# Inverting 16x16 diagonal blocks on POOL, reached by DMA, in a DeltaNet layer's kernel

## The chip, the cores and the metric

One core of a Trainium2 chip runs the whole layer. The metric is device time in microseconds of one execution; lower is better.

## The reference

The layer adds to its input an attention branch (a chunkwise delta rule, a multi-scale convolution and gates that mix them) and a feed-forward branch. Input and output are 2 x 4096 x 512, in float32; there are 4 heads of 128. The part that matters here is the delta rule: inside each chunk a unit lower triangular matrix is inverted by forward substitution.

```python
attn = -jnp.einsum('bhncd,bhned->bhnce', kbc, kc) * strict_lower
for i in range(1, chunk):
    upd = jnp.einsum('...j,...ji->...i', attn[..., i, :], attn[..., :, :i])
    attn = attn.at[..., i, :i].add(upd)
attn = attn + jnp.eye(chunk, dtype=q.dtype)
u = attn @ vc
w = attn @ kbc
```

The reference uses chunks of 32. The result does not depend on the size of the chunk but for rounding, and the kernel takes 128 tokens as a chunk.

## The kernel before, in words

The 4096 tokens of each of the 2 sequences (NB) are cut into NS = 32 steps of 128 tokens. The five engine programs, one function each (`sync_program`, `pool_program`, `tensor_program`, `scalar_program`, `vector_program`), are loops `for i in range(NS + 2)` in which step i is projected and transposed (f), step i - 1 is worked on in the middle (k) and step i - 2 is finished (c). Inside the loop every engine has its calls in an order that is written out by hand or by a planner, one call after another; for VectorE (DVE) this is down to single taps of the 31-tap convolution, `taps(s, h, lo, hi)`. Engines meet through semaphores alone. An engine never passes a call that waits.

A step has eight matrices (2 sequences x 4 heads) of 128x128. TensorE (PE) forms the Gram matrices K K^T in `gram` (L471), ScalarE (ACT) scales them into Bm in `scale_B` (L924), signal B_done. From Bm the inverse X of the unit triangular matrix is built in levels. Within 32x32 blocks there are five levels, block sizes 1 to 16. Level l is `inverse_W(s, l)` (L486): for eight matrices and four row groups a 32x32 by 32x16 product into the bank `inv`; on DVE `mask_W` (L1420) masks it into Wq; `inverse_Z(s, l)` (L509) multiplies by the transposed inverse so far, Xq; `step_Y` (L1428) subtracts the result from Yq, the inverse so far; and `turn_Y` (L1410) transposes Yq into Xq again. Level 0 needs no Z. Two more levels, from 32 to 64 (`inverse_W(s, 5)`, `copy_W`, `inverse_Z(s, 5)`, `spread_X`, `join_X`) and from 64 to 128 (`half_W`, `half_X`), complete X. X is used in `solve` (L557), which needs `subtract_state` and ends in u.

A float32 matmul of the program is two MATMUL records in the trace, so one W or Z pass of 32 matmuls is x64 there. PE does the level passes between other work: projections of the next step (`project`, L429), the transposes of x and of tokens (`turn_x`, `turn_tokens`), the last transposes of the output (`turn_o`) and its product (`attend`).

GpSimd (POOL) computes small powers: 1/sqrt for the layer norm (`deviation`), for q and k (`norms_q`, `norms_k`) and for the output norm (`invert_o`, L377). It also issues two sorts of accumulating DMA: `add_taps` (L385), which adds a product that ACT wrote into prod to my, and `add_out` (L390). SyncE (SP) issues loads: the weights, x of a step (`load_x`, L323), and a copy of x from DRAM to DRAM into the output (`copy_x`, L328), to which `add_out` adds.

Of the kernel before, what the change touches and what calls it, by code (L numbers as in the profile page):

```python
# [29 lines left out]
LEVELS = [1 << i for i in range(5)]  # L30
NL = len(LEVELS)
# [5 lines left out]
C_IDQ = C_LEV + NL * Q // 2  # L37
C_PART = C_IDQ + Q
# [35 lines left out]
def build(nc, x, out, w):  # L74
    NS = x.shape[1] // P
    with ExitStack() as ctx:
# [37 lines left out]
        def level_mask(l):  # L114
            k = LEVELS[l]
            m = cst[:, C_LEV + l * Q // 2:C_LEV + (l + 1) * Q // 2].rearrange("p (n k) -> p n k", k=k)
            return m[:, None, :, :].broadcast_to([P, NB * H, Q // 2 // k, k])

        def even(t, k):
            return t.rearrange("p (n k) -> p n k", k=2 * k)[:, :, 0:k]  # L120

        def evens(t, k):
            return t.rearrange("p b h (n k) -> p (b h) n k", k=2 * k)[:, :, :, 0:k]

        def ones_of(i):
            one = cst[:, C_IDQ:C_IDQ + Q].rearrange("p (n k) -> p n k", k=2)[:, :, i]
            return one[:, None, :].broadcast_to([P, NB * H, Q // 2])
# [17 lines left out]
        YW = sb("YW", P, NB, H, HP)  # L145
        S = sb("S", P, NB, D)
# [65 lines left out]
        def each_head(t):  # L212
# [27 lines left out]
        ones_in = signal("ones_in")  # L240
        W_mm, W_done, Wo_done = signal("W_mm", NL + 1), signal("W_done", NL), signal("Wo_done")
        Y_turned, X_spread, Z_mm, Y_done = (
            signal("Y_turned", NL), signal("X_spread"), signal("Z_mm", NL), signal("Y_done", NL))
# [40 lines left out]
        def sync_program(e):  # L284
# [48 lines left out]

            load(cst_in, cst[:, :], w["cst"])
# [4 lines left out]
            load_rest()  # L339
            for i in range(NS + 2):  # L340
                if 2 <= i < NS:
                    load_x(i)
                if 1 <= i <= NS:
                    copy_x(i - 1)
            for i in range(2):
                e.wait_ge(stored[i], NS // 2 * 16)

        def pool_program(e):
# [27 lines left out]

            def invert_o(s, b):  # L377
# [18 lines left out]
            for i in range(NS + 2):  # L396
# [10 lines left out]
                if k:  # L407
                    add_taps(i - 1, 3, 2)
                    add_taps(i - 1, 3, 3)
                    norms_q(i - 1)  # L410
                    norms_k(i - 1)
                if c:
                    add_out(i - 2)

        def tensor_program(e):
# [70 lines left out]
            def inverse_W(s, l):  # L486


                if l == 0:
                    e.wait_ge(*B_done.upto(s))  # L490
                    e.wait_ge(*aT_done.upto(s, 0))
                else:
                    e.wait_ge(*Y_done.upto(s, l - 1))
                for j in range(NB * H):
                    b, h = divmod(j, H)
                    if l < NL:
                        k, n = LEVELS[l], Q // 2
                        for r in range(4):
                            yv = Yq[rows(r), b, h, :] if l else cst[rows(r), C_IDQ:C_IDQ + Q]
                            i = e.matmul(inv[rows(r), j * n:(j + 1) * n].rearrange("p (n k) -> p n k", k=k),  # L500
                                         Bm[rows(r), b, h * P + r * Q:h * P + (r + 1) * Q], even(yv, k), start=True, stop=True)
                    else:
                        for r in (0, 2):
                            i = e.matmul(inv[rows(r + 1), j * Q:(j + 1) * Q],
                                         Bm[rows(r), b, h * P + (r + 1) * Q:h * P + (r + 2) * Q], Yq[rows(r), b, h, :],
# [270 lines left out]
        def scalar_program(e):  # L776
# [393 lines left out]
            for i in range(NS + 2):  # L1170
# [9 lines left out]
                if f:  # L1180
                    sum_x(i)
# [662 lines left out]
```

## Time and profile before

| what | us |
|---|---|
| median of the runs | 3586.57 |
| lowest and highest of 3 runs | 3575.02, 3588.57 |
| span of the profiled execution, first to last instruction | 3583.2 |
| PE busy | 3454.6 |
| DVE busy | 3199.5 |
| ACT busy | 2765.0 |
| POOL busy | 423.0 |

The time of the profiled execution itself is not given apart from its span; the median of the runs stands 3.4 us above the span. A row of the page's groups gives line, engine, operation, what is written and read, the count, then busy time in us and the mean of one in ns, and behind the last bar the idle time before them with what ended it. Line numbers are those of the kernel before.

### The profile page before, as it was taken

What the parts mean: (1) busy time and instruction counts of PE and PEld (TensorE: products, weight loads), DVE (VectorE), ACT (ScalarE), POOL (GpSimd) and SP (SyncE); (2) the same over time, 40 slices, a digit from 0 to 9 for tenths busy, and PEclk for the clock granted to TensorE, in tenths of its full rate; (3) what the DMA queues carried; (4) which work ended last, traced back from release to release, by engine and by line L of the source; (5) the groups of instructions that cost most, each with busy time, mean ns of one, the idle gap of its engine ahead of it and who ended that gap; (6) DMA issues with size and microseconds to landing.
All of it is one profiled execution on the core that took longest, in us unless ns stands there. A gap on an engine that the chain in (4) does not pass through costs nothing. (4 is left out here: it accounts for less than half of the span.)

```text
span 3583.2 us, 97697 instructions
## 1 busy us (share of the span) xinstructions
PE 3454.6 (96%) x37184; PEld 2572.7 (72%) x37184; DVE 3199.5 (89%) x8208; ACT 2765.0 (77%) x9176; POOL 423.0 (12%) x497
## 2 busy tenths in 40 slices
PE   6999999999999999999999999999999999999986
PEld 5677777777777777777777777777777777777764
DVE  6998898998989999989999989989999998899983
ACT  5677887778887778887788877788877788777774
POOL 1011100111100111101111001111001110011110
PEclk9999999999999999999999999999999999999988
DMA  5022111122111122111221111221112221112110
GB/s 177 5 41 42 35 31 28 31 41 42 30 32 25 38 42 40 31 28 26 41 42 37 30 28 31 41 41 30 32 22 41 42 38 29 31 27 41 36 26 10
DMA packets 52204, 131.04 MB, mean 37 GB/s; under 512 B 9389, under 2 KB 9901, under 8 KB 51481
## 3 DMA queue, kind: packets, MB, share of 16 engines
q0 software_dynamic: 31744, 79.70, 12.9%
q1 hardware_dynamic: 19992, 45.10, 3.7%
q8 instruction: 294, 4.82, 0.6%
q14 instruction: 174, 1.42, 0.1%
HBM read 45.09 MB, written 33.55 MB: 22 GB/s over the span
## 5 line engine op out<-in xcount | busy, mean ns | idle before, releaser
L1488 DVE SCALAR_TENSOR_TENSOR my<-vT,mw,my 128x256 f32<-128x256 f32 x5408 | 2230.9, 480 | 105.6 <-ACT my L1054 69.9
L645 PE MATMUL dense<-xsh,w 128*128 128x256 f32 x2048 | 481.9, 381 | 1.3
L645 PEld LDWEIGHTS dense<-xsh,w 128*128 128x128 f32 x2048 | 368.3, 190 | 68.9 <-ACT xr L1116 8.3
L388 POOL DMA_DIRECT2D my<-prod x160 | 141.8, 886 | 964.6 <-ACT my L1054 498.4
L439 PE MATMUL front<-xsh,wk 128*128 128x256 f32 x1024 | 239.9, 387 | 3.4 <-ACT raw L835 3.4
L439 PE MATMUL front<-xsh,wv 128*128 128x256 f32 x1024 | 240.9, 388 | 0.8 <-ACT xsh L812 0.8
L586 PE MATMUL dense<-xk,wfk 128*128 128x256 f32 x1024 | 239.5, 387 | 0.0
L357 POOL TENSOR_SCALAR vare<-xsq 128x2 f32<-128x2 f32 x32 | 6.1, 192 | 1951.3 <-ACT xsh L797 1951.3
L678 PE MATMUL dense<-wo,ms 128*128 128x512 f32 x512 | 235.7, 604 | 0.0
L598 PE MATMUL dense<-wr,xr 128*128 128x512 f32 x512 | 233.7, 599 | 1.2 <-DVE xb L1471 1.2
L1065 ACT ACTIVATE prod<-vT,mw 128x256 f32<-128x256 f32 x480 | 210.3, 511 | 28.2 <-DMA my<-prod 27.9
L439 PE MATMUL front<-xsh,wq 128*128 128x256 f32 x1024 | 231.9, 379 | 0.0
L602 PE MATMUL dense<-wfv,ka 128*128 128x512 f32 x512 | 230.2, 592 | 0.0
L623 PE MATMUL dense<-cm,ym 128*128 128x512 f32 x512 | 225.0, 592 | 0.0
L439 PEld LDWEIGHTS front<-xsh,wq 128*128 128x128 f32 x1024 | 191.9, 190 | 38.8 <-issue 14.8
L990 ACT ACTIVATE Bm<-cell,g 128x128 f32<-128x128 f32 x256 | 73.0, 368 | 184.7 <-PE cell L561 184.7
L439 PEld LDWEIGHTS front<-xsh,wk 128*128 128x128 f32 x1024 | 190.1, 190 | 29.9 <-ACT raw L835 3.5
L439 PEld LDWEIGHTS front<-xsh,wv 128*128 128x128 f32 x1024 | 190.7, 191 | 27.9 <-issue 1.4
L586 PEld LDWEIGHTS dense<-xk,wfk 128*128 128x128 f32 x1024 | 190.3, 191 | 27.0
L614 PE MATMUL small<-my,km 128*128 128x256 f32 x768 | 201.8, 400 | 2.2 <-issue 2.2
L1054 ACT ACTIVATE my<-vT,mw 128x256 f32<-128x256 f32 x384 | 167.4, 507 | 36.2 <-PE small L614 35.9
L602 PEld LDWEIGHTS dense<-wfv,ka 128*128 128x128 f32 x512 | 97.2, 190 | 122.5 <-issue 108.6
(181 smaller groups left out, 6897.8 us busy)
## 6 DMA issues: line engine op xcount, KB each, us to landing
my<-prod POOLq DMA_DIRECT2D x160, 384.0 KB, 4.1
xa<-in_x SPq DMA_DIRECT2D x32, 512.0 KB, 4.2
out<-xb POOLq DMA_DIRECT2D x32, 512.0 KB, 5.9
w<-in_w SPq DMA_DIRECT2D x1, 2048.0 KB, 17.1
wv<-in_wv SPq DMA_DIRECT2D x1, 1024.0 KB, 6.6
wk<-in_wk SPq DMA_DIRECT2D x1, 1024.0 KB, 8.9
wq<-in_wq SPq DMA_DIRECT2D x1, 1024.0 KB, 8.4
wfk<-in_wfkT SPq DMA_DIRECT2D x1, 1024.0 KB, 7.1
```

Of the source, the lines that this page charges most:

```text
L388: e.dma_start(my[h % 2][:, :, :], prod[:, :, :], accum_op=ALU.add).then_inc(taps_added, 16)
L439: i = e.matmul(by_batch(front[pair % 2][:, c * W:(c + 1) * W]), wt[:, k, hs(c0 + c)], xsh[s % 2][:, k, :, 1:1 + P], start=(k == 0), stop=( ...
L586: i = e.matmul(dense[pair][:, c * W:(c + 1) * W], wfk[:, k, hs(2 * pair + c)], xk[:, k, :], start=(k == 0), stop=(k == CB - 1))
L598: i = e.matmul(dense[0][:, :], xr[:, k, hs(b)], wr[:, k, :], start=(k == 0), stop=(k == CB - 1))
L602: i = e.matmul(dense[1][:, :], ka[:, k, hs(b)], wfv[:, k, :], start=(k == 0), stop=(k == CB - 1))
L614: i = e.matmul(s_mix, km[:, p, :], my[h % 2][:, p, :], start=(p == 0), stop=(p == 2))
L623: i = e.matmul(dense[b][:, :], ym[:, k, hs(b)], cm[:, k, :], start=(k == 0), stop=(k == CB - 1))
L645: e.matmul(by_batch(o), w1[:, k, hs(2 * pair + c)], xsh[s % 2][:, k, :, 1:1 + P], start=(k == 0), stop=False)
L678: i = e.matmul(dense[b][:, :], ms[:, b, hs(h)], wo[:, h, :], start=(h == 0), stop=(h == H - 1))
L1054: i = e.activation(by_batch(my[h % 2][:, p, :]), vT[s % 2][:, c, :, VH - TAPS[j] + 1:VH - TAPS[j] + 1 + P], ACT.Copy, scale=mw[:, WOFF[j] ...
L1065: i = e.activation(by_batch(prod[:, p, :]), vT[s % 2][:, c, :, off:off + P], ACT.Copy, scale=mw[:, col:col + 1])
L1488: i = e.scalar_tensor_tensor(o, vT[s % 2][:, c, :, off:off + P], mw[:, col:col + 1], o, ALU.mult, ALU.add)
```

## The change

The levels 1, 2, 4 and 8 of the inversion leave TensorE. Each 16x16 diagonal block (8 in each of 8 matrices, so 64, named UNITS) goes to one partition of its own and is inverted there on POOL by substitution. The way is through two new DRAM tensors whose matrices lie 129 rows apart, so that the diagonal blocks are evenly spaced:

```diff
+            def units(t):
+                each = t.rearrange("j p c -> (j p c)").rearrange("(m x) -> m x", x=UPITCH)
+                return each[:, 0:HQ * P].rearrange("m (r c) -> m r c", c=P)[:, :, 0:HQ]
...
+            def write_rows(s, b):
+                e.wait_ge(*B_done.upto(s, b))
...
+                e.dma_start(rows_out[b * H:(b + 1) * H, 0:P, :].rearrange("j p c -> p j c"), heads(Bm, b)).then_inc(rows_written, 16)
+            def read_rows(s):
+                e.wait_ge(rows_written, 16 * NB * (s + 1))
...
+                e.dma_start(Bu[:, :, :], units(rows_out)).then_inc(rows_read, 16)
+            def write_units(s):
+                e.wait_ge(*units_done.upto(s))
...
+                e.dma_start(units(units_out), Xu[:, :, :]).then_inc(units_written, 16)
+            def read_units(s):
+                e.wait_ge(units_written, 16 * (s + 1))
...
+                for r in range(4):
+                    e.dma_start(each_head(Yq)[rows(r), :, :],
+                                units_out[:, r * Q:(r + 1) * Q, r * Q:(r + 1) * Q].rearrange("j p c -> p j c")).then_inc(units_read, 16)
```

All of these are issued from SP. Its order in a pass of the loop is now:

```diff
+            zero_units()
             for i in range(NS + 2):
-                if 2 <= i < NS:
-                    load_x(i)
+                if 1 <= i <= NS:
+                    write_rows(i - 1, 0)
+                    write_rows(i - 1, 1)
+                    read_rows(i - 1)
+                if 1 <= i < NS - 1:
+                    load_x(i + 1)
                 if 1 <= i <= NS:
                     copy_x(i - 1)
+                    write_units(i - 1)
+                    read_units(i - 1)
```

POOL's part has 14 pairs of a product and a subtraction, of up to 56 elements in each of 64 partitions, and waits for each of its own results. It stands behind the DMA add of (3, 0) and ahead of that of (3, 1):

```diff
+            def invert_units(s):
+                def then(ins):
+                    e.wait_ge(*unit_step.link(ins))
+                e.wait_ge(rows_read, 16 * (s + 1))
...
+                then(e.tensor_tensor(Xu[:, :, :], Bu[:, :, :].rearrange("m j i -> m i j"), minus_lower, ALU.mult))
+                then(e.memset(Xu[:, :, :].rearrange("m i c -> m (i c)")[:, 0:HQ * HQ:HQ + 1], 1.0))
+                for j in range(1, HQ - 1):
+                    n = HQ - 1 - j
+                    then(e.tensor_tensor(Tu[:, 0:n, 0:j], Bu[:, j, j + 1:HQ][:, :, None].broadcast_to([UNITS, n, j]),
+                                         Xu[:, j, 0:j][:, None, :].broadcast_to([UNITS, n, j]), ALU.mult))
+                    left = e.tensor_tensor(Xu[:, j + 1:HQ, 0:j], Xu[:, j + 1:HQ, 0:j], Tu[:, 0:n, 0:j], ALU.subtract)
+                    if j < HQ - 2:
+                        then(left)
+                left.then_inc(units_done.sem, 1)
...
                     add_taps(i - 1, 3, 0)
+                    invert_units(i - 1)
                     add_taps(i - 1, 3, 1)
```

On PE one W and one Z pass are left (`inverse_W(s)`, waiting for units_read, and `inverse_Z(s)`), followed by `join_W` and `join_Z`, which were level 5. On DVE `turn_Y` runs twice, `mask_W` and `step_Y` once; ACT no longer writes ones into Yq:

```diff
-            def turn_Y(s, l):
+            def turn_Y(s, n):
+                if n:
+                    e.wait_ge(*Y_done.upto(s))
+                else:
+                    e.wait_ge(units_read, 64 * (s + 1))
...
-                e.transpose(flat(Xq), flat(Yq)).then_inc(Y_turned.sem, 1)
+                e.transpose(flat(Xq), flat(Yq)).then_inc(Y_turned.sem, 1)
```

The scratch of the software DMA queues is set to 8192 bytes. The orders of PE, ACT and DVE are all written anew. On PE, the calls from ffn_key(0) to solve(0) that opened a pass of the loop now close the one before, with key_state(0) ahead of solve(1). Of the order tables one line shows the kind:

```diff
-                    mask_W(i - 1, 3)
+                    taps(i - 1, 2, 39, 40)
```

PE from the second transpose of x to the third Z pass, in a pass of the loop before. cell<-qT,kT is query_key, front<-cst,xa turn_x, cell<-Yq,Bm a W pass, cell<-Wq,Xq a Z pass, cell<-S,kT key_state, small<-my,km kernel_mix, front<-xsh a projection:

```order
L426 MATMUL front<-cst,xa 128x128 x4
L500 MATMUL cell<-Yq,Bm 32x16 x32
L554 MATMUL cell<-S,kT 128x128 x4
L521 MATMUL cell<-Wq,Xq 32x16 x32
L614 MATMUL small<-my,km 128x256 x3
L500 MATMUL cell<-Yq,Bm 32x16 x32
L439 MATMUL front<-xsh,wv 128x256 x8
L521 MATMUL cell<-Wq,Xq 32x16 x32
L439 MATMUL front<-xsh,wv 128x256 x8
L500 MATMUL cell<-Yq,Bm 32x16 x32
L439 MATMUL front<-xsh,wk 128x256 x8
L521 MATMUL cell<-Wq,Xq 32x16 x32
```

The same place in the changed kernel, from the two query_key products to the one Z pass (turn<-cst,vT is turn_tokens, dense<-cst,dl turn_o):

```order
L545 MATMUL cell<-qT,kT 128x128 x8
L675 MATMUL small<-my,km 128x256 x3
L488 MATMUL front<-cst,xa 128x128 x4
L530 MATMUL turn<-cst,vT 128x128 x4
L615 MATMUL cell<-S,kT 128x128 x4
L501 MATMUL front<-xsh,wv 128x256 x16
L501 MATMUL front<-xsh,wk 128x256 x16
L530 MATMUL turn<-cst,vT 128x128 x4
L731 MATMUL dense<-cst,dl 128x128 x4
L555 MATMUL cell<-Yq,Bm 32x16 x32
L731 MATMUL dense<-cst,dl 128x128 x4
L566 MATMUL cell<-Wq,Xq 32x16 x32
```

The passes between the projections are gone, and the one W pass stands behind all four projections and the first turn_o.

DVE in the changed kernel, from the two masked attention matrices aT (`make_aT`) to the transpose that waits for units_read, the mask and the first subtraction; dl<-dl are the additions of the output's parts (`add_two`, `add_three`), my<-vT,mw,my are taps:

```order
L1440 TENSOR_TENSOR aT<-cell,cst 128x512 x2
L1515 SCALAR_TENSOR_TENSOR my<-vT,mw,my 128x256 x13
L1565 TENSOR_TENSOR dl<-dl,ms 128x512
L1515 SCALAR_TENSOR_TENSOR my<-vT,mw,my 128x256 x7
L1570 TENSOR_TENSOR dl<-dl,y 128x512
L1515 SCALAR_TENSOR_TENSOR my<-vT,mw,my 128x256 x2
L1565 TENSOR_TENSOR dl<-dl,ms 128x512
L1515 SCALAR_TENSOR_TENSOR my<-vT,mw,my 128x256
L1570 TENSOR_TENSOR dl<-dl,y 128x512
L1515 SCALAR_TENSOR_TENSOR my<-vT,mw,my 128x256 x17
L1453 STREAM_TRANSPOSE Xq<-Yq 128x256
L1460 TENSOR_TENSOR Wq<-cell,cst 128x128
```

Before, the first of five transposes stood directly behind the second aT.

SP in the changed kernel, the DMAs of one pass of the loop, with the semaphores that each waits for:

```order
L343 DMA rows_out<-Bm 128x4x128 [waits rows_read,B_done] x2
L349 DMA Bu<-rows_out 64x16x16 [waits units_done,rows_written]
L321 DMA xa<-in_x 128x2x512 [waits x_turned]
L327 DMA out<-in_x 2x4x16384
L357 DMA units_out<-Xu 64x16x16 [waits units_read,units_done]
L366 DMA Yq<-units_out 32x8x32 [waits Y_turned,X_spread,W_mm,units_written]
L366 DMA Yq<-units_out 32x8x32 x3
```

Before, only the load of x and the copy of x stood there.

## Rows read from the trace of the kernel before

**Rows 1.** The page's head and part 1, busy us (share of the span) and instructions.

```profile
span 3583.2 us, 97697 instructions
PE 3454.6 (96%) x37184; PEld 2572.7 (72%) x37184; DVE 3199.5 (89%) x8208; ACT 2765.0 (77%) x9176; POOL 423.0 (12%) x497
```

**Rows 2.** Timeline of PE (start us, us, ...), features' first transpose, steps 1 and 31.

```profile
154.58 0.22 PE L631 MATMUL small<-ident,fparts 128*108 128x128 bf16 x1
...
3425.14 0.27 PE L631 MATMUL small<-ident,fparts 128*108 128x128 bf16 x2
```

**Rows 3.** Groups by line, PE, Z and W passes of the levels.

```profile
L521 PE MATMUL cell<-Wq,Xq 32*32 32x16 f32 x8192 | 98.1, 182 | 24.1 <-issue 15.6 <-DVE Wq L1426 8.2
L500 PE MATMUL cell<-Yq,Bm 32*32 32x16 f32 x8192 | 97.3, 181 | 15.3 <-issue 12.1 <-DVE Yq L1438 2.8 <-DVE Yq L1434 0.3
```

**Rows 4.** Timeline of PE, a W pass between projections, and an attend.

```profile
1721.53 0.72 PE L500 MATMUL cell<-Yq,Bm 32*32 32x16 f32 x64
1722.19 3.73 PE L439 MATMUL front<-xsh,wk 128*128 128x256 f32 x16
...
1731.74 3.60 PE L678 MATMUL dense<-wo,ms 128*128 128x512 f32 x8
```

**Rows 5.** Timelines of ACT and PE, the second scaled Gram matrix and small groups.

```profile
1704.20 1.14 ACT L931 ACTIVATE Bm<-cell,g 128x128 f32<-128x128 f32 x4
...
1700.38 1.53 PE L614 MATMUL small<-my,km 128*128 128x256 f32 x6
...
1758.77 1.06 PE L554 MATMUL cell<-S,kT 128*128 128x128 f32 x8
```

**Rows 6.** Groups by line, DVE, transposes, masks and subtractions of the levels.

```profile
L1415 DVE STREAM_TRANSPOSE Xq<-Yq 128x256 f32<-128x256 f32 x160 | 70.2, 439 | 0.0
L1426 DVE TENSOR_TENSOR Wq<-cell,cst 128x128 f32<-128x128 f32 x160 | 44.8, 280 | 5.0 <-PE cell L500 4.9
L1438 DVE TENSOR_TENSOR Yq<-Yq,cell 128x128 f32<-128x128 f32 x128 | 36.2, 283 | 20.9 <-PE cell L521 20.9
```

**Rows 7.** DMA issues (KB each, us to landing), and SP's timeline of one.

```profile
km<-in_km SPq DMA_DIRECT2D x1, 192.0 KB, 2.5
mw<-in_m SPq DMA_DIRECT2D x1, 62.0 KB, 4.0
mu<-in_mu_k SPq DMA_DIRECT2D x1, 2.0 KB, 1.8
...
15.84 0.43 SPq L286 DMA_DIRECT2D mu<-in_mu_k  x1
```

**Rows 8.** Timelines of POOL and DVE, POOL beside taps and beside a resting DVE.

```profile
1723.25 0.48 DVE L1488 SCALAR_TENSOR_TENSOR my<-vT,mw,my 128x256 f32<-128x256 f32 x1
1723.38 0.40 POOL L379 TENSOR_SCALAR oe<-so 128x4 f32<-128x4 f32 x1
...
3561.47 0.18 POOL L379 TENSOR_SCALAR oe<-so 128x4 f32<-128x4 f32 x1 [70.23 <-ACT y L1156]
3561.73 1.03 POOL L383 TENSOR_TENSOR rro<-oe,cst 128x4 f32<-128x4 f32 x1
...
1745.19 9.19 DVE L1488 SCALAR_TENSOR_TENSOR my<-vT,mw,my 128x256 f32<-128x256 f32 x23
```

**Rows 9.** PE's timeline in the last step; busy time by stretch (us, then PE, PEld, DVE, ACT, POOL busy, PEclk, DMA share, GB/s).

```profile
3460.86 1.05 PE L521 MATMUL cell<-Wq,Xq 32*32 32x16 f32 x64 [1.92 <-DVE Wq L1426]
3464.75 1.05 PE L500 MATMUL cell<-Yq,Bm 32*32 32x16 f32 x64 [2.83 <-DVE Yq L1438]
3469.85 1.05 PE L521 MATMUL cell<-Wq,Xq 32*32 32x16 f32 x64 [4.05 <-DVE Wq L1426]
...
3476.20 4.28 PE L678 MATMUL dense<-wo,ms 128*128 128x512 f32 x8
...
1700.00:1810.00 110.00, 107.69 (x1168) 80.21 (x1168) 99.90 (x259) 86.88 (x288) 13.44 (x16) 1.00 0.17 34
3460.00:3470.00 10.00, 2.26 (x141) 2.10 (x145) 9.96 (x26) 9.86 (x38) 4.46 (x6) 0.53 0.45 81
```

More of the change, by code:

```diff
@@ L29 @@
 Q = 32
-LEVELS = [1 << i for i in range(5)]
-NL = len(LEVELS)
+HQ = Q // 2
+NU = P // HQ
+UNITS = NU * NB * H
+PITCH = (P + 1) * P
+UPITCH = HQ * (P + 1)
 WOFF = [0, TAPS[0] * CB, (TAPS[0] + TAPS[1]) * CB]
@@ L682, in tensor_program @@
                 f, k, c = i < NS, 1 <= i <= NS, i >= 2
-                if c:
-                    turn_tokens(i - 2, 3)
-                    inverse_Z(i - 2, 5)
-                    ffn_key(i - 2, 0)
-                    half_W(i - 2)
-                    ffn_key(i - 2, 1)
-                    half_X(i - 2)
-                    ffn_out(i - 2, 0)
-                    solve(i - 2, 1)
-                    key_state(i - 2, 0)
-                    kernel_mix(i - 2, 2)
-                    solve(i - 2, 0)
                 if k:
@@ L731, in tensor_program @@
                     kernel_mix(i - 1, 0)
+                    gram(i - 1, 0)
                     gram(i - 1, 1)
-                    query_key(i - 1, 0)
                 if f:
@@ L736, in tensor_program @@
                 if k:
-                    turn_tokens(i - 1, 2)
-                    inverse_W(i - 1, 0)
+                    query_key(i - 1, 0)
                     query_key(i - 1, 1)
+                    kernel_mix(i - 1, 1)
                 if f:
@@ L773, in tensor_program @@
                 if k:
-                    inverse_W(i - 1, 5)
+                    join_Z(i - 1)
+                    ffn_key(i - 1, 0)
+                    half_W(i - 1)
+                    ffn_key(i - 1, 1)
+                    half_X(i - 1)
+                    ffn_out(i - 1, 0)
+                    key_state(i - 1, 0)
+                    solve(i - 1, 1)
+                    kernel_mix(i - 1, 2)
+                    solve(i - 1, 0)
         def scalar_program(e):
@@ L1556, in vector_program @@
                 if c:
+                    taps(i - 2, 3, 4, 5)
+                    taps(i - 2, 3, 2, 4)
+                    taps(i - 2, 3, 7, 8)
+                    taps(i - 2, 3, 5, 6)
+                    taps(i - 2, 3, 10, 11)
+                    taps(i - 2, 3, 6, 7)
+                    taps(i - 2, 3, 13, 14)
+                    taps(i - 2, 3, 9, 10)
+                    taps(i - 2, 3, 8, 9)
+                    taps(i - 2, 3, 16, 17)
                     taps(i - 2, 3, 12, 13)
-                    taps(i - 2, 3, 10, 11)
+                    taps(i - 2, 3, 19, 20)
@@ L1702, in vector_program @@
                 if k:
-                    taps(i - 1, 2, 16, 17)
+                    taps(i - 1, 2, 29, 30)
+                    taps(i - 1, 2, 18, 19)
                 if c:
@@ L1706, in vector_program @@
                 if k:
-                    taps(i - 1, 2, 19, 20)
+                    taps(i - 1, 2, 16, 17)
                 if c:
@@ new lines, in vector_program @@
+                    taps(i - 1, 2, 45, 46)
+                    turn_Y(i - 1, 0)
+                    mask_W(i - 1)
+                    taps(i - 1, 2, 46, 47)
+                    taps(i - 1, 2, 33, 34)
+                    taps(i - 1, 2, 47, 48)
+                    taps(i - 1, 2, 28, 29)
+                    taps(i - 1, 2, 48, 49)
+                    taps(i - 1, 2, 36, 37)
+                    step_Y(i - 1)
+                    taps(i - 1, 2, 49, 50)
+                    turn_Y(i - 1, 1)
+                    taps(i - 1, 2, 50, 51)
```

565 lines of the change are left out of this document (263 added, 302 removed).

## The prediction

> **What bounds the kernel now.** I read the page's totals first [rows 1]: PE is busy 3454.6 of 3583.2 us (96%), DVE 3199.5 (89%), and the others less. PE is nearly full and in its own order, so a step of the pipeline costs what PE issues in it plus what PE waits for. The timeline of PE gives the step [rows 2]: the first transpose of features (L631) starts at 154.58 and, 30 steps later, at 3425.14, so a step is 3270.56 / 30 = 109.0 us. Then I read PE's groups by line [rows 3] for what the inversion costs there, PE's timeline at the passes [rows 4], and the timelines of ACT, DVE and POOL for what the new way would cost [rows 5 to 8]. A difference under 0.5% (18 us) is about what a measurement of this kernel can't tell from none.
>
> **What goes from PE.** Five passes W of 64 instructions and four passes Z stand in each step; one of each stays. A pass holds PE from one start to the next: 1721.53 to 1722.19, that is 0.66 us [rows 4]. Seven passes are 7 x 0.66 = 4.6 us. PE also idles before these passes: 24.1 + 15.3 = 39.4 us in 32 steps [rows 3], 1.2 us a step, and a little before the first W; I take 1.1 us of it. The step would be 109.0 - 4.6 - 1.1 = 103.3 us if nothing took their place.
>
> **What goes from DVE and ACT.** Three of five transposes, four of five masks and all but one subtraction. By their groups [rows 6]: 3/5 of 70.2, 4/5 of 44.8 and 3/4 of 36.2 are 105.1 us, and the first subtraction of each step, another 32 of the last kind, makes it 114 us or 3.6 us a step. ACT loses the ones that it wrote into Yq, under half a microsecond. Neither engine is the bound, so this buys room alone. The larger order tables redistribute taps and other work; I cost the move of the first ten PE calls from the head of one pass of the loop to the end of the one before at nothing, since the same instructions stand in the same sequence (only key_state(0) and solve(1) change places). The added buffers' zeroing is one DMA in the first 45 us of loads, where PE waits anyway.
>
> **What comes: one long chain.** From the second scaled gram (B_done) to the first pass W everything is now serial: Bm to DRAM, the blocks to 64 partitions, POOL, the inverses to DRAM, and four DMAs to Yq. Its price, link by link:
> - *Bm out*, 256 KB. No row shows a plain store from SBUF. The nearest load is 192 KB in 2.5 us; below stands 1.8 for 2 KB, above 4.0 [rows 7]. I take 2.6.
> - *Blocks in*, 64 KB in 1024 runs of 64 bytes. The floor is 1.8 us, a 2 KB load; above is 4.0, a 62 KB load of 512 short runs that stood behind others [rows 7]. I take 3.0.
> - *Inverses out*, the same runs: 3.0, same bounds.
> - *Inverses in*, four DMAs, issued one by one. An issue takes 0.43 us (mu_k's on SP [rows 7]), so the last starts after 1.3 and lands 2.1 later: 3.4. Bounds: 1.3 + 1.8 and 1.3 + 4.0.
> - *Between them*, four semaphores at about 0.1 each: 0.4.
> - *POOL*: a product over 256 elements, a memset, then 28 operations in pairs, each waiting for the one before. The nearest small POOL operation is TENSOR_SCALAR: 0.18 us while DVE rests, but 0.40 while DVE runs taps, and it ends 0.05 us after the tap that was running (tap 1723.25 to 1723.73, POOL done 1723.78) [rows 8]. The next dependent one starts 0.08 later (3561.65 to 3561.73). So a dependent POOL operation gets one opening per tap, and taps follow each other every (9.19 - 0.48) / 22 = 0.396 us [rows 8]. 28 x 0.40 = 11.2, plus 1.1 for the first two: 12.3. Bounds: undisturbed, 28 x (0.18 + 0.08) + 0.6 = 7.9; two taps for each, 28 x 0.79 + 1.5 = 23.6. I take the middle value because rows 8 show exactly this waiting, on operations as short.
>
> Sum 2.6 + 3.0 + 12.3 + 3.0 + 3.4 + 0.4 = **24.7 us**, between 15 and 40 at the ends.
>
> The Trainium skill, "DMA: Bandwidth & Descriptors", section "Anatomy of one DMA", puts about 2.0 us of fixed cost on a DMA and little on 64 KB, but its "Specifications" add read-modify-write under 512 bytes. By the fixed cost alone the estimate of the four links is 2.6 + 2.2 + 2.2 + 3.5 = 10.5 us, 1.5 less than mine, and the total some 45 us lower; the second rule speaks against this change, and no row here shows a short store.
>
> **What covers it.** ACT ends the second scaled gram at 1704.20 + 1.14 = 1705.34 [rows 5]. By the new order PE then has up to the first pass W: kernel_mix 1.53; half of query_key, turn_x, turn_tokens, key_state, turn_tokens and turn_o, six small groups of 128x128 matmuls of which the fullest takes 1.06 and the halves about 0.5, 3.6 in all; and four projections at 3.73, which overlap their neighbours by some 0.08, 14.6 [rows 4, 5]. That is 19.7 us. So PE waits 24.7 - 19.7 = **5.0 us** in each step. DVE's order agrees: 40 taps and four additions stand between the last aT and the transpose that waits for the same DMAs, 40 x 0.396 + 4 x 0.6 = 18.2 us; behind that transpose DVE's taps wait too, in the room that [rows 6] give and DVE's idle 384 us. Part of the 5 us comes already at turn_o: POOL's third product add, both inverse roots of o and so ACT's normalize_o are queued behind the 30 POOL instructions. SP's load and copy of x stand between blocks in and inverses out, but they issue while POOL computes.
>
> **What the wait costs beside itself.** In the last step, where PE idles 2 to 4 us before passes [rows 9], the granted clock was 0.53 between 3460 and 3470, nearly all of it at 1.2 GHz in place of 2.4, and the attend group that follows takes 4.28 us, against 3.60 in a full step [rows 4, 9]. In a full step it is 1.00 [rows 9]. I add 1.5 us a step for matmuls behind the wait at the lower level; bounds 0 and 3.6.
>
> **Sum.** 103.3 + 5.0 + 1.5 = 109.8, or +0.8 us a step over 31 steps with cover: +25. In the last step no projections cover the chain: PE waits 14.6 more, while before it already waited for level passes, 1.92 to 4.05 before each of three, about 9 [rows 9], and later for the tap DMAs; I add 20 for it with the later tap adds. 3583 + 45 = 3628 us; the runs' median stands 3.4 above this span, and the profiled execution's own time isn't told apart, so I name **3630**, 1.2% above the median of 3586.57.
>
> **The rivals.**
> 1. *The chain fits, or nearly.* If POOL runs as while DVE rests (7.9) and the DMAs take 2 us each, the chain is under 20 and PE stays at 103.3: 3583 - 31 x 5.7 + 5 = 3411; with a wait of 3 us about 3505. For it: the removed 4.6 us are certain, and a wait under some 4 us leaves a gain. Against it: rows 8, DVE is never at rest there. Chance 0.33, all of it faster.
> 2. *The wait eats just the gain.* Wait and clock together between 4.6 and 5.7 us, which with the last step's 20 us is within 18 us of before. Chance 0.12.
> 3. *My forecast*, a net loss of 0.1 to 4.4 us a step, with the last step's 20 us 3605 to 3740: chance 0.38.
> 4. *DVE becomes the bound.* In a full step it is busy 99.90 of 110 us [rows 9], so 99.0 of 109.0, with 10 idle; without 3.6 busy and 0.8 of waits for passes it is 104.6. If each of 28 POOL operations held DVE off for its 0.18 and DVE waited 5.0 at the transpose, the step is 104.6 + 5.0 + 5.0 = 114.6, total 3583 + 31 x 5.6 + 20 = 3777. Against it: taps beside POOL's roots keep 0.48 [rows 8]. For it: these read far fewer elements than 40 on average. It decides from 0.18 us per operation. Chance 0.09. The Trainium skill, "SBUF — State Buffer", section "Who interferes with whom", says that a DVE instruction with two SBUF inputs and a GpSimd one that reads SBUF exclude each other for the whole instruction, whoever starts first. The trace agrees in one direction, POOL waiting for the tap (0.40 against 0.18); by that rule taps wait too, and it is this rival.
> 5. *POOL falls behind by a tap each time*: 23.6 in place of 12.3, wait 16.3, 3583 + 31 x 12.1 + 40 = 3998. Chance 0.08.
>
> So faster 0.33, same 0.12, slower 0.55. The range reaches from the chain that fits, 3410, to the edge of the DVE case, 3770; below and above lie rival 5 and the ends of the others.
>
> **What would show it.** Right: PE idle before the first pass W (and before turn_o), released by a DMA into Yq or by DVE's transpose, 3 to 8 us a step; POOL's 28 operations 0.32 to 0.42 us each; the two short-run DMAs landing in 2.5 to 3.5 us; taps still 0.48; granted clock under 1.00 in full steps. Wrong: steps of 103 to 105 us with no wait at W (rival 1); taps over 0.5 us and DVE busy over 3150 (rival 4); POOL operations at 0.8 (rival 5). Seven fewer passes and PE busy down by about 150 us should show in any case.

## The result, and the profile after

The changed kernel takes 3790.15 us (median of 4 runs, 3788.75 to 3791.78), beside 3587.51 us for the kernel before (4 runs): ratio 1.0575, 95% interval 1.0558 to 1.0591. It is slower, as forecast, by 203 us in place of 43, and 20 us above the upper end of the range. Of all executions in what follows, one of ten of the version with the roots of o earlier took 7909.89 us; why is not known, and the ratios leave it out.

The page's head and part 1 of the changed kernel:

```profile
span 3787.5 us, 69932 instructions
PE 3383.6 (89%) x22848; PEld 2490.8 (66%) x22848; DVE 3165.3 (84%) x7856; ACT 2761.4 (73%) x9144; POOL 813.6 (21%) x1457
```

Against [rows 1] PE issues 14336 matmuls fewer, yet its busy time falls by 71 us alone, and the span grows by 204.3. Measured from one first transpose of features to the next over 30 steps, as in [rows 2], a step is 115.4 us in place of 109.0. Summed over PE's timeline in those 30 steps, the idle time per step is 10.1 us, before 1.7; all figures "a step" below are taken this way. The waits view, PE and ACT (engine, line waited for: us in total, times, longest us):

```profile
PE dense L731 <- ACT dl L1203: 117.6, 24, 12.6
PE turn L530 <- ACT turn L945: 101.8, 23, 21.0
PE cell L555 <- DMA Yq<-units_out: 66.1, 27, 12.1
...
ACT dl L1203 <- POOL rro L443: 97.1, 24, 7.8
```

L731 is turn_o, L530 turn_tokens, L555 the first pass W. The three stand one behind another in PE's order, and a step has its wait at one or another of them. Two steps in PE's timeline:

```profile
1705.59 0.60 PE L530 MATMUL turn<-cst,vT 128*128 128x128 f32 x4
1714.01 1.12 PE L731 MATMUL dense<-cst,dl 128*128 128x128 f32 x4 [7.82 <-ACT dl L1203]
1716.72 1.05 PE L555 MATMUL cell<-Yq,Bm 32*32 32x16 f32 x64 [1.59 <-DMA Yq<-units_out]
...
1720.80 5.98 PE L739 MATMUL dense<-wo,ms 128*128 128x512 f32 x8
...
1727.33 3.70 PE L739 MATMUL dense<-wo,ms 128*128 128x512 f32 x8
...
1831.10 1.08 PE L530 MATMUL turn<-cst,vT 128*128 128x128 f32 x4 [7.31 <-ACT turn L945]
...
1833.22 1.05 PE L555 MATMUL cell<-Yq,Bm 32*32 32x16 f32 x64
```

In the first step PE waits 7.82 us at turn_o and 1.59 at W; in the second 7.31 us at turn_tokens, and then nothing. Together the three make 7.9 us a step. The first attend behind a wait takes 5.98 us, the second 3.70. The stretches of the second step (PE, PEld, DVE, ACT, POOL busy, PEclk, DMA share, GB/s) show the granted clock at 0.60 right behind the wait, most of it at 1.2 GHz:

```profile
1820.00:1830.00 10.00, 3.79 (x18) 2.98 (x16) 6.65 (x16) 4.36 (x22) 7.53 (x20) 0.89 0.24 48
1830.00:1840.00 10.00, 8.90 (x147) 5.82 (x148) 6.11 (x17) 8.86 (x29) 1.91 (x2) 0.60 0.41 71
```

POOL's timeline of that step: the second product add, the product with the mask, the memset, the first and the last of 28 operations, then the two kinds of work that queued behind them.

```profile
1809.99 0.86 POOL L448 DMA_DIRECT2D my<-prod  x1 [6.56 <-ACT my L1095]
1811.53 1.93 POOL L426 TENSOR_TENSOR Xu<-Bu,cst 64x256 f32<-64x256 f32 x1 [0.68 <-DMA Bu<-rows_out]
1813.52 0.12 POOL L427 MEMSET Xu<- 64x16 f32 x1
1813.72 0.50 POOL L430 TENSOR_TENSOR Tu<-Bu,Xu 64x14 f32<-64x14 f32 x1
1814.29 0.34 POOL L432 TENSOR_TENSOR Xu<-Xu,Tu 64x14 f32<-64x14 f32 x1
...
1826.08 0.32 POOL L432 TENSOR_TENSOR Xu<-Xu,Tu 64x14 f32<-64x14 f32 x1
1827.45 0.87 POOL L448 DMA_DIRECT2D my<-prod  x1 [1.05 <-ACT prod L1106]
1828.40 0.19 POOL L439 TENSOR_SCALAR oe<-so 128x4 f32<-128x4 f32 x1
```

From 1811.53 to 1826.40 the inversion takes 14.9 us. The DMA issues (KB each, median us to landing), and two of DVE's groups:

```profile
my<-prod POOLq DMA_DIRECT2D x160, 384.0 KB, 4.4
...
rows_out<-Bm SPq DMA_DIRECT2D x64, 256.0 KB, 3.5
...
Yq<-units_out SPq DMA_DIRECT2D x128, 32.0 KB, 2.0
...
Bu<-rows_out SPq DMA_DIRECT2D x32, 64.0 KB, 3.0
units_out<-Xu SPq DMA_DIRECT2D x32, 64.0 KB, 3.4
```

```profile
L1515 DVE SCALAR_TENSOR_TENSOR my<-vT,mw,my 128x256 f32<-128x256 f32 x5408 | 2233.8, 483 | 52.4 <-DMA my<-prod 40.9
...
L1453 DVE STREAM_TRANSPOSE Xq<-Yq 128x256 f32<-128x256 f32 x64 | 28.3, 442 | 218.7 <-DMA Yq<-units_out 218.7
```

Taps take 483 ns, as in the kernel before (0.48 in [rows 8]), so DVE isn't held off for whole operations. It waits 218.7 us at the transpose for the inverses, more than PE does at W.

Medians over 27 full steps, from the issue and landing times in the trace, give the chain from B_done: 0.4 to the second write's issue, 3.6 until it has landed, 3.0 blocks in, 14.8 POOL, 3.4 inverses out, 3.6 inverses in: 28.8 us. The first pass W starts 0.1 later, in all 29.0 us after B_done.

### The profile page after: what moved, and what is told of

The parts are those of the page before. It is cut to its first block, busy times and chain, and to the rows that moved or that the text cites. A ratio compares the mean times of both kernels' runs of the same rounds, so it can differ in the third digit from the quotient of the medians.

```text
span 3787.5 us, 69932 instructions
## 1 busy us (share of the span) xinstructions
PE 3383.6 (89%) x22848; PEld 2490.8 (66%) x22848; DVE 3165.3 (84%) x7856; ACT 2761.4 (73%) x9144; POOL 813.6 (21%) x1457
## 3 DMA queue, kind: packets, MB, share of 16 engines
q0 software_dynamic: 31744, 79.70, 12.3%
## 4 chain that ended last, share of the span: by engine, by line
PE 48%; ACT 20%; DMA 12%; POOL 9%; issue 8%; DVE 2%; SPq 1%; ACTq 0%; POOLq 0%; DVEq 0%
PE dense L739 8%; PE dense L706 6%; PE dense L647 6%; PE dense L659 6%; PE dense L663 6%; POOL Xu L432 4%; POOL Tu L430 4%; PE front L501 3%; DMA my<-prod 3%; DMA rows_out<-Bm 3%; DMA units_out<-Xu 2%; DMA Bu<-rows_out 2%; PE small L675 2%; ACT my L1095 2%; ACT dense L1125 2%
## 5 line engine op out<-in xcount | busy, mean ns | idle before, releaser
L739 PE MATMUL dense<-wo,ms 128*128 128x512 f32 x512 | 288.9, 716 | 0.0
L501 PE MATMUL front<-xsh,wv 128*128 128x256 f32 x1024 | 231.9, 384 | 15.1 <-ACT xsh L860 15.1
L501 PE MATMUL front<-xsh,wk 128*128 128x256 f32 x1024 | 226.7, 379 | 0.0
L501 PEld LDWEIGHTS front<-xsh,wq 128*128 128x128 f32 x1024 | 192.0, 190 | 38.8 <-issue 14.8
L1453 DVE STREAM_TRANSPOSE Xq<-Yq 128x256 f32<-128x256 f32 x64 | 28.3, 442 | 218.7 <-DMA Yq<-units_out 218.7
L739 PEld LDWEIGHTS dense<-wo,ms 128*128 128x128 f32 x512 | 113.0, 233 | 126.4 <-issue 123.9
L675 PE MATMUL small<-my,km 128*128 128x256 f32 x768 | 194.0, 389 | 1.5 <-DVE my L1515 1.5
```

Source lines behind the costliest of these rows:

```text
L501: i = e.matmul(by_batch(front[pair % 2][:, c * W:(c + 1) * W]), wt[:, k, hs(c0 + c)], xsh[s % 2][:, k, :, 1:1 + P], start=(k == 0), stop=( ...
L675: i = e.matmul(s_mix, km[:, p, :], my[h % 2][:, p, :], start=(p == 0), stop=(p == 2))
L739: i = e.matmul(dense[b][:, :], ms[:, b, hs(h)], wo[:, h, :], start=(h == 0), stop=(h == H - 1))
```

## The experiments

I began with two suspects. One is the chain. The other is SP's copy of x into the output: 512 KB in 8 packets of 64 KB, 2.4 us each and two at a time, about 10 us in all. Before the change they run 46 to 57 us after the step's first product add, clear of all five adds; now, placed behind the read of the blocks, they run at 12 to 22 us, beside the second add. That add then lands after 10 to 16 us in two thirds of the steps instead of 4, and ACT's next product waits for it, ahead of copy_tokens and so of turn_tokens. ACT's timeline in the second step above:

```profile
1825.60 1.31 ACT L1106 ACTIVATE prod<-vT,mw 128x256 f32<-128x256 f32 x3 [7.90 <-DMA my<-prod]
```

**The copy behind the chain.** The copy goes behind the reads of the inverses in SP's order.

```diff
-                    copy_x(i - 1)
                     write_units(i - 1)
                     read_units(i - 1)
+                    copy_x(i - 1)
```

> The changed kernel with SP's copy of x (DRAM to DRAM) issued after the four DMAs into Yq instead of before the inverses go out. Theory 1, the serial chain from the scaled gram to Yq (28 us against some 20 of cover) makes the wait: the waits of PE before turn_tokens, turn_o and W, 7.9 us a step together, fall by at most 2, the step stays 113 to 115.5 us, ratio to before 1.035 to 1.06. Theory 2, the copy's 64 KB packets hold DMA engines, the tap add (3, 0) lands after 10 to 16 us instead of 4 and ACT and PE wait for that: adds land in 4 to 6 us again and most of the 7.9 us goes, step 106 to 109, ratio 0.97 to 1.00. Both agree that the wait at turn_tokens (2.7 us a step on average) goes.

3923.42 us, ratio 1.0963 [1.0944, 1.0982], slower still. The copy's packets now run at 30 to 42 us, beside the fourth add, which lands after 12 to 13 us: some 110 of its 128 packets start in its first 4 us, the last ones only when the copy's last packet is through. Rows of PE's timeline:

```profile
1772.56 1.12 PE L731 MATMUL dense<-cst,dl 128*128 128x128 f32 x4 [6.00 <-ACT dl L1203]
1775.68 1.05 PE L555 MATMUL cell<-Yq,Bm 32*32 32x16 f32 x64 [2.01 <-DMA Yq<-units_out]
...
1794.89 1.14 PE L598 MATMUL cell<-YW,Bm 64*64 64x64 f32 x16 [1.41 <-ACT YW L1010]
```

The wait at turn_tokens is gone, as both theories had it, but 6.0 and 1.9 us a step stand at turn_o and W, the same sum. The collision moved to another place, where it costs a new wait, 2.2 us a step at L598 (join_W's product). Neither theory's time held.

**POOL's 28 operations left out.** In invert_units only the product and the memset remain, so the inverse is incomplete and only the time counts.

```diff
-                for j in range(1, HQ - 1):
...
-                left.then_inc(units_done.sem, 1)
```

> The changed kernel without POOL's 28 products and subtractions (the masked product and the memset stay), so the inverse is left incomplete. Theory 1: the chain is 13 us shorter, 15 to 16 us, and covered: no wait at turn_o or W, clock 1.00 in full steps, step 103 to 105.5, ratio 0.95 to 0.97. Theory 2: the tap add (3, 0) still lands after 10 to 16 us in two thirds of the steps and PE still waits about 7 us before turn_tokens in some of them, step 106 to 108, ratio 0.975 to 0.99.

3709.83 us, ratio 1.0346 [1.0314, 1.0379], step 113.2, above both expectations. Only 2 us a step are won by taking 13 us out of POOL's part of the chain. PE still waits 3.1 us a step at turn_tokens and 3.0 at W. The DMA issues say why:

```profile
units_out<-Xu SPq DMA_DIRECT2D x32, 64.0 KB, 12.6
```

The inverses are now written while the copy's packets still run on the same queue, and land after 12.6 us in place of 3.4. The inverses reach Yq only 3 us earlier.

**The copy moved in the kernel before.** There the copy alone is put where the change puts it.

```diff
-                if 2 <= i < NS:
-                    load_x(i)
+                if 1 <= i < NS - 1:
+                    load_x(i + 1)
                 if 1 <= i <= NS:
                     copy_x(i - 1)
```

> The kernel before with SP's copy of x issued right behind the next load of x, where the changed kernel has it, and nothing else. Theory 2: the tap add that runs beside it lands after 10 to 16 us, ACT waits for it, 0.5 to 4 us a step, ratio 1.005 to 1.04. Rival, POOL's new operations delay its own DMA's descriptors: adds land in 4 to 6 us here, ratio 0.995 to 1.005.

3712.42 us, ratio 1.0365 [1.0347, 1.0382]: the copy's place is able to cost 130 us in a kernel without any chain. The second add lands after 6 to 10 us there. ACT's timeline shows a product held 4.49 us by an add, and PE waits for ACT at the third projection:

```profile
1781.61 1.31 ACT L1065 ACTIVATE prod<-vT,mw 128x256 f32<-128x256 f32 x3 [4.49 <-DMA my<-prod]
```

```profile
PE front L439 <- ACT raw L835: 82.5, 30, 4.5
```

**POOL alone.** The same 30 operations once more at the program's start, on a zeroed Bu, while DVE rests.

```diff
+            probe()
             for i in range(NS + 2):
```

> The changed kernel with POOL's 30 operations run once more at its start, on zeros, while DVE rests. If taps of DVE stretch POOL's operations, as forecast from rows 8: here the product over 256 elements takes 0.6 to 0.9 us instead of 1.89, the 28 others 0.20 to 0.30 each, 28 with gaps 8 to 9.5 us instead of 13. If POOL's own pace sets them: the same as in the loop, 1.9 and 0.2 to 0.36, 12 to 13 us. The time itself changes by under 15 us either way.

3791.98 us in its one run. POOL's timeline:

```profile
4.38 0.84 POOL L463 TENSOR_TENSOR Xu<-Bu,cst 64x256 f32<-64x256 f32 x1
...
5.48 0.21 POOL L467 TENSOR_TENSOR Tu<-Bu,Xu 64x14 f32<-64x14 f32 x1
5.76 0.23 POOL L469 TENSOR_TENSOR Xu<-Xu,Tu 64x14 f32<-64x14 f32 x1
...
14.60 0.21 POOL L469 TENSOR_TENSOR Xu<-Xu,Tu 64x14 f32<-64x14 f32 x1
```

Alone the whole takes 14.81 - 4.38 = 10.4 us, in the loop 14.8. At the start the other engines rest too, so this run by itself does not name DVE; the loop does. Of the 896 operations of the 28 in the changed kernel's trace, 20 have no DVE instruction beside them and take 0.25 us on average, the others 0.38. So working beside DVE costs POOL 4.4 us a step. Undisturbed, POOL still needs 0.33 us per operation, start to start.

**The copy first.** The copy stands ahead of the first write of rows, so it goes once an older output is stored, as before the change.

```diff
                 if 1 <= i <= NS:
+                    copy_x(i - 1)
                     write_rows(i - 1, 0)
...
-                    copy_x(i - 1)
```

> The changed kernel with SP's copy of x put ahead of the first write of B's rows, so that it goes once the output two steps before is stored, clear of the five adds of the taps' products, as it did in the kernel before. POOL's inversion and all five transfers of the chain stay. Theory (two causes: the copy's place costs some 4 us a step, the chain the rest): the add (3,0) lands in 4 to 5 us again, PE's wait ahead of turn_tokens(3) falls under 1 us a step, the step is 111 to 113 us and the time 3640 to 3710, ratio to the kernel before 1.015 to 1.035. Rival (the chain of the inverses is all, the copy only took the blame): the wait stands ahead of W, Z or turn_o instead, 3760 to 3800, ratio 1.05 to 1.06. Rival (the prediction was right but for the copy): 3610 to 3650, ratio 1.01 to 1.02.

3788.74 us, ratio 1.0574 [1.0554, 1.0594]. The packets run at 52 to 63 us, the second add lands in 5 to 8 us, and nothing is won: the theory of two separate costs fell. PE's waits:

```profile
PE dense L731 <- ACT dl L1203: 200.9, 32, 12.6
PE cell L555 <- DMA Yq<-units_out: 68.5, 32, 11.5
```

The 7.9 us are all there, now in every step as 6.0 at turn_o and 1.9 at W.

**The copy in rows.** It stays in the change's place, but goes as 2 KB rows.

```diff
-                e.dma_start(out[:, s * P:(s + 1) * P, :], x[:, s * P:(s + 1) * P, :])
+                e.dma_start(out[:, s * P:(s + 1) * P, :].rearrange("b p d -> p b d"),
+                            x[:, s * P:(s + 1) * P, :].rearrange("b p d -> p b d"))
```

> The changed kernel with the copy of x at the same place, but cut into rows of 2 KB (128 tokens by 2 batches), where the changed kernel's copy moves 8 packets of 64 KB of some 2.4 us each. Theory (it is the few large packets, one behind another on few DMA engines, that hold back the packets of the add beside them): spread over 16 engines the copy takes 3 to 5 us, the add (3,0) lands in 4 to 8 us, ratio to the kernel before 1.02 to 1.04. Rival (bytes count, not packets: the memory or the engines are full for as long whatever the packets): the copy takes as long, the add lands after 10 to 16 us still, ratio 1.05 to 1.06. Rival (many small packets fill the queue ahead of the inverses' transfer): inverses out lands after 6 us or more, ratio over 1.06.

3782.41 us, ratio 1.0554 [1.0535, 1.0573]. The copy lands after 7.3 us, no add takes more than 8.3, the inverses out 3.4: the large packets do hold the others back, as the theory said, but its 1.02 to 1.04 missed, for their removal again changes only where PE waits. Two different cures of the copy leave the time as it was, within 8 us.

**Both taken away.** The copy first, and POOL's 28 operations left out, so the inverse is incomplete here too.

> The copy put first as in the run above, and POOL's 28 subtractions and products of the inversion left out (the blocks then hold the unit matrix minus B, not the inverse). Theory (copy's place and chain are the whole loss): both gone, the step is 103 to 105 us, the time 3410 to 3480, ratio to the kernel before 0.95 to 0.97. Rival (a third cost remains, such as the transfers of 64-byte runs beside the adds, or the order of the engines): a step over 107 us, ratio 0.98 or more.

3460.45 us, ratio 0.9656 [0.9640, 0.9672]. PE's timeline, where turn_o and W stood:

```profile
1669.40 0.66 PE L723 MATMUL dense<-cst,dl 128*128 128x128 f32 x4
1669.99 0.73 PE L547 MATMUL cell<-Yq,Bm 32*32 32x16 f32 x64
...
1672.03 0.71 PE L558 MATMUL cell<-Wq,Xq 32*32 32x16 f32 x64 [0.73 <-DVE Wq L1452]
```

No wait is left there but 0.73 us at Z for DVE's mask. The four kernels make a square (us a step):

| | copy in the change's place | copy first |
|---|---|---|
| all 28 operations | 115.4 | 114.9 |
| none | 113.2 | 104.8 |

Taking away one gives 0.4 or 2.1 us, both 10.6. Copy and chain are two ways to the same instructions of PE, about equally late, and the later one counts. They are not fully apart: without the operations, the copy in the change's place also holds up the chain itself, at the inverses out (12.6 us above). With the copy out of the way this run also measures the cover: its inverses land 15.2 us after the second write's issue, but W starts at 19.8, so PE has 19.8 + 0.4 = 20.2 us of work between B_done and W.

**Half of the operations.** The copy first, and only the last 7 pairs; the blocks are not fully inverted.

```diff
-                for j in range(1, HQ - 1):
+                for j in range(HQ // 2, HQ - 1):
```

> The copy of x first, and of POOL's 14 pairs only the last 7 (j from 8 to 14), so that the blocks aren't fully inverted. Theory (the wait is the chain minus a cover of 20.2 us from the second scaled gram to the first pass): 14 operations fewer at 0.46 us shorten the chain from 28.7 to 22.2 us, PE's waits at turn_o and W fall from 7.9 to some 2 us, the step is 106.5 to 108.5 us (114.9 with all pairs, 104.8 with none) and the ratio to the kernel before 0.98 to 1.00. Rival (the wait at turn_o is not the chain, but POOL's later work, the clock is most of the rest): step 104.8 to 106, ratio 0.965 to 0.975. Rival (something else holds the end): step 110 us or more.

3600.51 us, ratio 1.0049 [1.0033, 1.0064], step 109.3, above the 108.5 of the theory. The chain was nearly as computed (the inverses land 22.3 us after the second write's issue, 22.7 after B_done), and so were the waits:

```profile
PE cell L555 <- DMA Yq<-units_out: 74.3, 32, 6.5
PE dense L731 <- ACT dl L1203: 28.3, 13, 12.6
```

That is 2.7 us in a step of the loop. The rest goes with the clock. PE's step without its idle time, and the time at 1.2 GHz in the step, are 102.0 and 0.2 us without the wait, 104.5 and 6.4 here, 105.0 and 12.1 with all operations, the copy first in all three. Beside a wait of 2.7 us PE's own work takes 2.5 us longer, beside one of 7.9 us 3.0.

**POOL's other work put into the inversion.** The add (3,1) goes after 8 pairs, the roots of o, merged into one, after 10; PE, ACT and DVE keep their orders.

> The copy of x first, the whole inversion, and POOL's other work put into its middle: the add (3,1) after 8 of 14 pairs, both roots of o as one pair of operations after 10. PE, ACT and DVE keep their orders. Theory (the chain alone sets how long PE is late, the work queued behind it only says at which instruction): the wait at turn_o goes to under 1 us, that at W grows to 9 to 11 us since the chain is 2.9 us longer, the step is 116 to 118 us, ratio 1.065 to 1.085. Rival (the wait at turn_o is a cost of its own): step 109 to 111, ratio 1.0 to 1.02.

3885.78 us, ratio 1.0841 [1.0823, 1.0859], step 118.3.

```profile
PE cell L562 <- DMA Yq<-units_out: 244.1, 32, 12.7
PE dense L738 <- ACT dl L1210: 135.3, 32, 14.5
```

The chain grew by 3.2 us, the two waits by 3.4, the step by 3.4: what stands at turn_o is paid back at W. The theory had the time right and the places not: the wait at turn_o only fell to 3.9 us, not under 1, and that at W is 7.5, not 9 to 11.

**The passes later on PE.** Both turn_o, both attend and half of ffn_key go ahead of W; ACT's and DVE's orders follow.

```diff
+                    ffn_key(i - 1, 0, (0,))
                     inverse_W(i - 1)
+                    ffn_key(i - 1, 0, (1,))
                     inverse_Z(i - 1)
+                    ffn_key(i - 1, 1, (0,))
                     join_W(i - 1)
+                    ffn_key(i - 1, 1, (1,))
                     join_Z(i - 1)
...
                     half_W(i - 1)
...
                     half_X(i - 1)
+                    project(i, 4)
```

> The same POOL order, and the passes behind the chain put later on PE: both turn_o, both attend and half of ffn_key stand ahead of W, halves of ffn_key between the passes, the parts of ffn_out between the half passes, the fifth projection of the next step ahead of key_state, the second gate matmul ahead of outputs; ACT's and DVE's orders follow. Theory (the chain of 31.6 us then has a cover of 20.2 + 9.3 + 1.9 = 31.4 us): PE idles 2 to 4 us a step, the clock stays at the full one, the step is 104 to 107 us and the time 3430 to 3530, ratio 0.955 to 0.985, faster than both kernels. Rival (all later work of the step moves with the chain, since ACT and DVE are near full too): new waits of PE at key_state, solve or outputs, the step 109 us or more, ratio over 1.0.

3743.80 us, ratio 1.0446 [1.0431, 1.0462], step 113.6: 46 us better than the change, far off the 3430 to 3530 expected. No wait is left at the passes, since W starts 4 us after the inverses land. Most of what is left, 4.2 us a step, is at turn_o; as the rival said, new waits came as well, 1.3 us at kernel_mix and 0.9 at solve.

```profile
PE dense L743 <- ACT dl L1214: 145.7, 47, 14.5
```

**The roots of o earlier.** They stand after 7 pairs, where ACT's squares are just done; some smaller moves on ACT and DVE.

```diff
-                    if j == 9:
+                    if j == 7:
                         add_taps(i - 1, 3, 1)
-                    if j == 11 and c:
+                    if j == 8 and c:
                         invert_o(i - 2)
```

> The kernel of the run before (passes put later on PE) with three small moves: POOL takes the add (3,1) after 6 pairs and the roots of o after 7 instead of 10, as soon as ACT's squares of o are there; ACT scales v ahead of the half W's copy and copies kernel_mix 2 between the two copies of o; DVE subtracts the state of batch 0 two taps earlier. Theory (the 4.2 us left ahead of turn_o were the roots' place in POOL's queue alone, since W now has 4 us of room): PE's wait at turn_o falls under 1.5 us, the waits of 1.3 us at kernel_mix and 0.9 us at solve go, the step is 105 to 107.5 us and the time 3450 to 3540, ratio 0.965 to 0.985, faster than both kernels. Rival (the room at W was not real, W's wait returns in the same size): step 110 to 113 us, ratio over 1.02.

3590.12 us, ratio 1.0011 [0.9996, 1.0025]: no difference to the kernel before, 200 us better than the change. The step is 108.6 us, over the 107.5 expected and under the rival's 110. The wait at turn_o is 1.7 us, and 1.3 us of the step stand at 1.2 GHz. A larger part than I had counted is PE's own time, 103.2 us without idle time against 102.0.

```profile
PE dense L743 <- ACT dl L1214: 67.6, 61, 14.5
```

**The squares first.** Four more moves on ACT, POOL and DVE.

> The kernel of the run before with four more moves: ACT squares o ahead of the products for add (3,1), DVE's second sum of o stands one tap earlier, POOL takes the roots ahead of that add, and ACT makes the products for add (3,2) after mix_half instead of before, so that mix_in and with it ffn_key are ready earlier. Theory (the 2.6 us that PE still waits at turn_o and ffn_key hang on ACT's order alone): both waits together fall to 1 to 1.6 us, the step is 107 to 107.8 us, the ratio to the kernel before 0.985 to 0.995. Rival (ACT only swaps one late result for another): the taps' adds come later, DVE waits for them, the step stays at 108.3 to 109 us and the ratio at 1.00.

3619.97 us, ratio 1.0119 [1.0102, 1.0136]. The wait at turn_o did fall, to 0.8 us, but the fourth add came later, and DVE waited for it ahead of its step at Y, which PE's join waits for:

```profile
PE cell L582 <- DVE Yq L1475: 50.7, 32, 6.6
PE dense L654 <- DVE xk L1501: 45.3, 32, 7.2
```

```profile
1765.12 0.88 DVE L1525 SCALAR_TENSOR_TENSOR my<-vT,mw,my 128x256 f32<-128x256 f32 x2 [3.61 <-DMA my<-prod]
```

The rival's mechanism held, at a price above its own 108.3 to 109: the step is 109.7 us. No version here with all of the inversion beats the kernel before.

## Where the prediction was right, and where it was wrong

**The mechanism was right, its size was not.** The step that failed is the size of the wait: a chain of 24.7 us against a cover of 19.7, so 5.0 us a step. Measured are 28.8 against 20.2, and 7.9 us. Two smaller terms failed beside it, the clock's price and the new orders' cost of nothing. PE waits for one long chain at turn_o and at W, POOL's later work is queued behind the inversion, the taps keep their 0.48 us, and the gain in passes is lost. The run with both taken away shows it: without the wait the step is 104.8 us, with it 114.9.

**The cover**, 19.7 us, measured 20.2. Right.

**The passes.** I took 4.6 us and 1.1 of idle time off the step. PE's time without idle is 107.3 before and 102.0 in the run without a wait, 5.3 less (PE stands 0.6 us less at 1.2 GHz, which is in it). The idle time doesn't fall by 1.1 but rises by that much, 2.8 against 1.7. I had forecast 103.3 for a step without the wait; it is 104.8. The idle times before the passes did go, as forecast, but others took their place that the kernel before doesn't have: 0.7 us at Z for the mask, 0.7 where a small product waits for xr (L716 in that run), and 0.9 at turn_x, a projection and another product of xsh. The prediction put the new orders of calls at nothing; which of the moves makes these waits was not tested. That 1.5 us, 45 us in 30 steps, is the first part of the 160 that the forecast lacks.

**The chain was mis-sized, the step that failed most.** 24.7 us predicted, 28.8 measured. Link by link: Bm out 2.6 with its part of the semaphores, measured 0.4 + 3.6; blocks in 3.0 and 3.0; inverses out 3.0 and 3.4; inverses in 3.4 and 3.6; POOL 12.3 and 14.8. On POOL the sentence "a dependent POOL operation gets one opening per tap" was nearly right: two thirds of the 28 operations stand 0.38 to 0.44 us apart. But about one in six takes 0.5 to 0.8, which makes 0.45 on average in place of 0.40, 1.4 us in all; and the product and the memset, costed at 1.1 us, take 2.2 (the product 1.93 in the step shown). The lower bound of 7.9 was wrong as well: alone the sequence takes 10.4, so rival 1, with a chance of 0.33, rested on a price that POOL did not reach even undisturbed. The transfers were short by 1.6 us, 1.0 of it at Bm out, which no row had shown. The wait is then 28.8 - 20.2 = 8.6 by sums and 7.9 by PE's idle time; since PE then waits no more at Z (0.7 us), the idle time of a step grows by 7.2 from the run without a wait to the one with it, not by 5.0: 2.2 us a step, 66 us.

**What the wait costs beside itself**, 1.5 us, measured 3.0 between the runs with all operations and none, inside the bound of 3.6: 45 us. The half kernel shows why an average was the wrong way to take it: this price is nearly whole at a wait of 2.7 us already.

**SP's copy**, "they issue while POOL computes", was costed at nothing. It was read from the issue, and not from the transfer, which takes 10 us and delays an add beside it. Alone in the kernel before it costs 3.65%. In the changed kernel it costs 0.4 us a step, 12 us, because the chain is late by as much; with POOL's operations left out it costs 8.5 (113.2 against 104.8). That this hole in the argument hardly moved the result was luck.

**The ends.** Of the span's 204.3 us, 30 x 6.36 = 191 lie in the 30 steps, 13.6 before and behind them, where I had 20 + 0.8. Per step, then: -5.3 and +1.1, +7.2 for the wait, +3.0 of clock, +0.4 of the copy, together +6.4 where I had +0.8. The four parts make 45 + 66 + 45 + 12 = 168 us, less 7 at the ends: the 160 us that lay between forecast and result.

**The rivals.** Not 1, 2 or 5. The loss of 6.4 us a step also lies past the 0.1 to 4.4 that the forecast gave its own case. Rival 4's 3777 us is the nearest to the time, by coincidence: its mechanism, DVE held off by POOL for whole operations, is excluded, for taps take 483 ns, and with copy and operations both taken away PE waits for DVE for 0.8 us a step. Its test "DVE busy over 3150" was badly chosen, for the busy time is 3165.3 all the same: the groups of [rows 6] did fall by 114 us (42 + 36 + 27 + 9), as forecast, but part of that lay beside their neighbours, the taps follow each other every 0.408 us in place of 0.401, some 39 us in all, and the four sums of o per step take 0.76 us in place of 0.69, so the busy time falls by 34 alone.

The rule of the Trainium skill, "SBUF — State Buffer", section "Who interferes with whom", showed here mostly on one side: POOL pays 4.4 us a step beside DVE, while taps inside the inversion start every 0.42 us, outside every 0.40. As to runs under 512 bytes, for which the Trainium skill, "DMA: Bandwidth & Descriptors", section "Specifications", has a read-modify-write: the 64 KB in runs of 64 bytes took 3.4 us out and 3.0 in, and 256 KB in runs of 512 bytes 3.5. With POOL's other work put into the inversion, with the passes later and with the squares first the same 64 KB store took 2.5. No run changes the length of a run alone, so a price of it is not shown; these figures leave little room for a large one.

Of the signs that the prediction named, the wait of 3 to 8 us came (7.9), and so did the short-run DMAs at 2.5 to 3.5 (3.0, 3.4). POOL's operations, at 0.32 to 0.42 us, came at 0.45 from start to start, and PE's busy time, down by 150, fell by 71, since the matmuls behind the waits run slower; without the wait it falls by 5.3 us a step.

**What stays open.** Why the version with the passes later needs 1.2 us more of PE's own time was not separated. Groups cut in half and the clock both lie in it, but the last version has 103.0 us against 102.0 with only 0.5 us of the step at 1.2 GHz against 0.2, so there the clock can't be most of it. An inversion with a second partition per block or fewer operations was not tried.

## What to carry to other kernels

Work moved off a full engine into a chain through other engines is worth what the chain's length leaves under the work that covers it, so measure both in one trace, B_done to use. A lone resource, a queue of POOL or SP, should be asked for everything that stands behind the new work and for how long its transfers run, not when they are issued. Where two causes lead to the same wait, taking away either shows almost nothing; only the square of both shows what each is worth.

## What the runs showed of the hardware

- A DRAM-to-DRAM copy of 512 KB that goes as 8 packets of 64 KB, two at a time, takes 10 us. Transfers beside it land late: an add of 384 KB after up to 16 us in place of 4, a 64 KB store behind it on SP's queue after 12.6 in place of 3.4. In 2 KB rows the same copy lands after 7.3 us and no add takes over 8.3.
- A dependent POOL operation over 14 to 56 elements in 64 partitions takes 0.21 to 0.30 us alone, a product over 256 elements 0.84. Beside DVE's taps the first takes 0.34 in the median and up to 0.70, the second 1.93 in the step shown.
- In the half kernel PE waits 2.7 us a step, 6.4 us of the step are at 1.2 GHz, and PE's own work takes 2.5 us longer than without the wait. With all operations and the copy first it waits 7.9 us, 12.1 are at 1.2 GHz, and the price is 3.0.
